# First attention of a two-layer block: probabilities times context, then Wv, instead of V; two kinds of transposition moved from TensorE to DMA

## What is computed

```python
q = (x @ Wq + bq)            # 16 heads of 128
k = (ctx @ Wk + bk)          # 4 key heads of 128, each used by 4 query heads
v = (ctx @ Wv + bv)          # 4 value heads of 128
q, k = rmsnorm(q), rmsnorm(k)
probs = softmax(q @ k.T / sqrt(128) + mask)
x = x + (probs @ v) @ Wo
```

## Time and profile before

| | us |
|---|---|
| runs of the kernel before, median (lowest to highest) | 5748.51 (5746.48 to 5749.6) |
| the profiled execution | 5724.92 |
| its span in the profile | 5723.2 |
| busy in the span: TensorE matmul | 4635.3 (81%) |
| TensorE weight load | 3681.8 (64%) |
| VectorE | 3950.1 (69%) |
| ScalarE | 2792.3 (49%) |
| GpSimd | 1760.5 (31%) |

### The profile page before, as it was taken

The page is one execution under the profiler, slowest core; times in us unless marked ns, Lnnn a source line. Parts: engine busy times, 40 slices in busy tenths (PEclk is TensorE's granted clock), DMA queues, the critical chain, the costliest instruction groups (busy, mean ns, idle before and its releaser), DMA issues. The chain is left out here.

```text
span 5723.2 us, 119501 instructions
## 1 busy us (share of the span) xinstructions
PE 4635.3 (81%) x39954; PEld 3681.8 (64%) x39955; DVE 3950.1 (69%) x7266; ACT 2792.3 (49%) x5207; POOL 1760.5 (31%) x2107
## 2 busy tenths in 40 slices
PE   4679999999999999999997407743888888888865
PEld 2447777777777777777776306632666666666654
DVE  4757777777777777777764633356777777777767
ACT  2335555555555555555543133321666666666643
POOL 2544444444444444444430163344000000000003
PEclk9789999999999999999998659975999998989976
DMA  5222112112212211221204274444333333333320
GB/s 191 89 62 57 38 49 57 50 42 52 52 41 51 57 48 44 52 52 40 52 27 122 76 217 124 124 128 116 93 86 87 83 87 81 90 78 89 89 52 24
DMA packets 395261, 436.41 MB, mean 76 GB/s; under 512 B 184225, under 2 KB 352801, under 8 KB 384526
## 3 DMA queue, kind: packets, MB, share of 16 engines
q1 hardware_dynamic: 366558, 388.13, 26.2%
q0 software_dynamic: 9216, 22.03, 1.2%
q10 hardware_dynamic: 19008, 19.40, 1.0%
HBM read 187.81 MB, written 144.83 MB: 58 GB/s over the span
## 5 line engine op out<-in xcount | busy, mean ns | idle before, releaser
L1804 DVE TENSOR_SCALAR_CACHE_REDUCE b_pr<-b_ps 112x1500 f32<-112x1500 f32 x256 | 439.3, 1716 | 279.4 <-PE b_ps L1879 279.1
L701 POOL TENSOR_TENSOR a_ksq<-a_kb 125x512 f32<-125x512 f32 x384 | 399.0, 1039 | 708.8 <-DVE a_kb L651 708.5
L616 ACT ACTIVATE a_pTh<-a_pt 125x448 f16<-125x448 f32 x768 | 402.7, 543 | 326.0 <-PE a_pt L775 321.4
L1761 ACT ACTIVATE b_pTh<-b_pt 125x448 f16<-125x448 f32 x768 | 392.7, 542 | 340.4 <-PE b_pt L1892 336.3
L673 DVE CUSTOM_DVE_ANT_0 a_pr<-a_ps,a_mask 112x1500 f32<-112x1500 f32 x256 | 439.7, 1718 | 164.7 <-PE a_ps L112 162.8
L110 PE MATMUL a_po<-a_vh,a_pTh 125*112 125x128 f16 x3072 | 549.5, 220 | 3.7 <-DVE a_pTl L689 3.1
L112 PE MATMUL a_po<-a_vh,a_pTl 125*112 125x128 f16 x3072 | 547.4, 219 | 0.0
L111 PE MATMUL a_po<-a_vl,a_pTh 125*112 125x128 f16 x3072 | 547.0, 219 | 0.0
L1811 DVE TENSOR_TENSOR b_pTl<-b_pt,b_pTh 125x448 f16<-125x448 f32 x768 | 454.0, 616 | 72.6 <-ACT b_pTh L1761 69.2
L1892 PE MATMUL b_pt<-ident,b_pr 112*125 112x112 f32 x3072 | 474.4, 294 | 32.0 <-DVE b_pTl L1811 26.9
L1997 POOL PARTITION_ALL_REDUCE f_ma<-f_mx x1 | 0.4, 374 | 1588.3 <-DVE f_mx L2057 1588.3
(11 more groups left out here) (376 smaller groups left out, 13470.8 us busy)
## 6 DMA issues: line engine op xcount, KB each, us to landing
b_ks<-b_kn SPq DMA_DIRECT2D x384, 187.5 KB, 4.4
scratch_cT<-a_cT SPq DMA_DIRECT2D x128, 375.0 KB, 3.1
b_cT<-scratch_cT SPq DMA_DIRECT2D x32, 1500.0 KB, 6.9
a_ctx<-ctx SPq DMA_DIRECT2D x32, 1440.0 KB
scratch_yd<-e_y SPq DMA_DIRECT2D x88, 256.0 KB, 2.1
scratch_xd<-q_zero ACTq DMA_DIRECT2D x4, 4736.0 KB
scratch_o<-a_ot SPq DMA_DIRECT2D x64, 224.0 KB
m_ot<-scratch_o SPq DMA_DIRECT2D x16, 896.0 KB
```

The source lines that it names most:

```text
L616: nc.scalar.activation(pTh[:, r % 2, 4 * third:4 * third + 4].rearrange("p k c -> p (k c)"), ps_t[n % 2][0:KP, 0:4 * RP], ACT.Copy).then_i ...
L701: nc.gpsimd.tensor_tensor(ksq[:, kt % 2], kb[0:KP, kt % 4], kb[0:KP, kt % 4], ALU.mult).then_inc(s["k_squared"], 1)
L1804: nc.vector.tensor_scalar(pr[:, n % 2].rearrange("p (a k) -> p a k", k=500), ps_s[0:RP, :, 0:500], -1.0, None, ALU.mult, ALU.min, accum_ou ...
```

## The change

Only the first attention and what reads its results are rewritten.

- There is no V any more. With the probabilities turned, step `P` (24 per batch, 12 matmuls of 224 columns each) multiplies them by the context itself, giving for each key head and its two rounds a mix of 256 features by 224 rows (`a_pa`). Step `G` splits this into `a_ah`, `a_al`, step `O` multiplies it by Wv (6 matmuls of 224 columns, 4 times per batch), and step `Z` adds bv and splits the result in f16, already turned, into `a_ot`. One store per two batches writes `scratch_oT`.
- The probabilities are scaled by one over the sum and split in their untransposed form: `H` on ScalarE and `L` on VectorE, each over 112x1500 from SBUF, 8 per batch. Then SyncE issues two DMA transpositions per round, from SBUF to SBUF (112 rows of 1536 f16 values).
- The context is loaded in four pieces of three rows per partition, split by `D` (ScalarE and GpSimd, 125x768, 4 per batch), and turned by four DMA transpositions per batch (128 rows of 1536 values). It is kept in f16 for three batches, since `P` needs it.
- TensorE loses `C`, `U`, `T`, `V` and keeps `K`, `R`, `S`. Key norms run over two tiles at once. GpSimd has an order of its own. The helper `rounds` writes six batches into one pass of the loop, 4 passes.
- `mix0_phase` loads the turned, split result directly and has no `turn_o` and no `split_o`.
- The second attention reads `scratch_cT` in another layout with 128 keys per tile; its matmul counts stay.

```diff
 ORDER0 = {
     "tensor": """
-        S0 T23< K0 V21< C1 V22< V23< T0 U0 K1 T1 T2 C2 S1 R0 U1 V0 V1 K2 C3 T3 T4 U2 R1 S2 V2 C4 T5 K3 V3 R2 V4
...
+        P17< K0 S0 K1 P18< S1 P19< K2 K3 S2 R0 O2< P20< P21< P22< K4 K5 P23< R1 S3 P0 R2 P1 P2 P3 K6 P4 R3 K7
+        S4 R4 P5 K8 S5 K9 P6 R5 S6 P7 P8 P9 P10 O3< R6 K10 O0 K11 R7 S7 P11 R8 P12 P13 R9 P14 P15 P16 O1 R10
+        R11""",
     "scalar": """
...
+        S0 H0 S1 H1 R0 Z2< S2 H2 D0 D1 G3< R1 R2 S3 H3 R3 D2 D3 R4 G0 S4 H4 S5 R5 H5 S6 Z3< R6 H6 Z0 R7 G1 R8
+        S7 R9 H7 Z1 R10 R11 G2""",
     "vector": """
...
+        S0 K1 I0 Q0 S1 L0 K2 I1 K3 S2 L1 R0 Q1 Z2< I2 K4 K5 L2 S3 G3< R1 Q2 R2 I3 K6 L3 R3 K7 S4 R4 G0 K8 I4
+        Q3 S5 L4 K9 I5 R5 S6 L5 Q4 I6 Z3< R6 K10 L6 Z0 K11 R7 S7 Q5 G1 R8 I7 R9 L7 Z1 R10 R11 G2 K0>""",
+    "gpsimd": """
+        D0 D1 N2 q6 D2 q7 D3 N3 q8 q9 N4 q10 q11 N5 q0> q1> N0> q2> q3> N1> q4> q5>""",
...
 def attn0_phase(nc, g, io):
...
+            def turn_ctx(tile, half):
...
+                wait(sp, s["work_done"], NW * (G - 1) + AT["K", HT * half + HT - 1] + 1)
+                passed(sp, sp_gate)
+                wait(sp, kept[half], 16 * G)
+                passed(sp, sp_gate)
+                sp.wait_ge(s["c_lo"], 4 * G + 2 * half + 2)
+                passed(sp, sp_gate)
+                for n, c in enumerate((ch, cl)):
+                    sp.dma_start_transpose(out=cT[:, n, part].rearrange("p k c q -> p (k c) q"),
+                                           in_=c[:, k, part].rearrange("q k d -> q (k d)")).then_inc(c_turned[half], 16)
...
+            def turn(tile, r):
+
+                G, h, k = tile[0], r // 2, r % 2
+                wait(sp, s["mix_done"], NKV * G + h - 1)
+                passed(sp, sp_gate)
+                for n, (p, pT, ready) in enumerate(((ph, pTh, "p_hi"), (pl, pTl, "p_lo"))):
+                    sp.wait_ge(s[ready], NR * G + r + 1)
+                    passed(sp, sp_gate)
+                    sp.dma_start_transpose(out=pT[:, h % 2, :, k], in_=p[:, k].rearrange("q k c -> q (k c)"))\
+                        .then_inc(turned[n][k], 16)
...
+                elif kind == "H":
+                    act.wait_ge(s["inv_ready"], NR * b + n + 1)
+
+                    wait(act, turned[0][n % 2], 16 * (NKV * b + n // 2))
+                    nc.scalar.activation(ph[:, n % 2, :, 0:KP], pr[:, n % 2].rearrange("p (k c) -> p k c", c=KP),
+                                         ACT.Copy, scale=inv[:, par, n:n + 1]).then_inc(s["p_hi"], 1)
...
                 if kind == "S":
                     dve.wait_ge(s["scores_done"], NR * b + n + 1)
+
+                    wait(dve, s["p_lo"], NR * b + n - 1)
...
+                elif kind == "L":
+                    dve.wait_ge(s["p_hi"], NR * b + n + 1)
+
+                    wait(dve, turned[1][n % 2], 16 * (NKV * b + n // 2))
+                    nc.vector.scalar_tensor_tensor(pl[:, n % 2, :, 0:KP],
+                                                   pr[:, n % 2].rearrange("p (k c) -> p k c", c=KP),
+                                                   inv[:, par, n:n + 1], ph[:, n % 2, :, 0:KP], ALU.mult,
+                                                   ALU.subtract).then_inc(s["p_lo"], 1)
...
+                elif kind == "P":
+                    h, c, third = n // 6, n // 3 % 2, n % 3
+                    ring, _ = of_three(batch)
+                    if n % 6 == 0:
+
+                        wait(pe, s["mix_lo"], NKV * b + h - 1)
+                        for t in turned:
+                            for k in range(2):
+                                pe.wait_ge(t[k], 16 * (NKV * b + h) + 16)
+                    for kt in range(4 * third, 4 * third + 4):
+                        feat = slice(c * 128, c * 128 + 128)
+                        last = three_products(nc, ps_a[h % 2][:, c], ch[0:KP, ring, kt, feat], cl[0:KP, ring, kt, feat],
+                                              pTh[0:KP, h % 2, kt].rearrange("p r q -> p (r q)"),
+                                              pTl[0:KP, h % 2, kt].rearrange("p r q -> p (r q)"),
+                                              start=(kt == 0), stop=(kt == KT - 1))
...
 def mix0_phase(nc, g, io):
...
-                wait(sp, s["oT_done"], 4 * t - 4)
-                sp.dma_start(ot[:, k, :], io.o0[ds(t * TT, TT), :]).then_inc(o_in[k], 16)
+                wait(sp, s["y_done"], t - 1)
+                sp.dma_start(oT[:, k].rearrange("p n h q -> p (n h q)"),
+                             io.oT[ds(t, 1)].rearrange("a p n h q -> p (a n h q)")).then_inc(o_in[k], 16)
```

More of the change, by code:

```diff
@@ L459, in batches, with moved, rounds, turn @@
         turn((g_, g_ % 2, g_ // 2))
+RING = 3
+ROUND = 2 * RING
+def moved(tile, d):
+    n, k, i = tile
+    return n + d, (k + d) % ROUND, i + (k + d) // ROUND
+def rounds(eng, steps, attend, work):
+    def turn(batch):
+        for kind, n, off in steps:
+            lead = {"D": 2, "K": 1, "R": 1, "q": 1, "N": 1, "Q": 1}.get(kind, 0)
+            at = moved(batch, off + lead)
+            if exists(at, B):
+                (work if lead else attend)(kind, n, at)
+    count = (B - 4) // ROUND
+    for b in (-2, -1, 0):
+        turn((b, b % ROUND, b // ROUND))
+    with eng.Fori(0, count) as i:
+        for k in range(1, ROUND + 1):
+            turn((ROUND * i + k, k % ROUND, i + k // ROUND))
+    for b in range(ROUND * count + 1, B + 1):
+        turn((b, b % ROUND, b // ROUND))
+def of_two(tile):
+    n, k, i = tile
+    return k % 2, RING * i + k // 2
+def of_three(tile):
+    n, k, i = tile
+    return k % RING, 2 * i + k // RING
 def attn0_phase(nc, g, io):
@@ new lines, in store, with load, step @@
+            def store(pair):
+                sp.wait_ge(s["o_taken"], 2 * NKV * pair + 2 * NKV)
+                passed(sp, sp_gate)
+                sp.dma_start(io.oT[ds(pair, 1)].rearrange("a p n h q -> p (a n h q)"),
+                             ot[:].rearrange("p n h b q -> p (n h b q)")).then_inc(stored, 16)
+            def load(tile, p):
+                if exists(tile, B):
+                    load_ctx(tile, p)
+            def step(tile):
+                after, second = moved(tile, 1), moved(tile, 2)
+                more = exists(second, B)
+                turn(tile, 0)
+                turn(tile, 1)
+                if exists(after, B):
+                    load_q(after)
+                turn(tile, 2)
+                load(second, 2)
+                load(second, 3)
+                turn(tile, 3)
+                if more:
+                    turn_ctx(second, 0)
+                turn(tile, 4)
+                turn(tile, 5)
+                if more:
+                    keep_ctx(second, 0)
+                if tile[1] % 2 == 0 and not (isinstance(tile[0], int) and tile[0] == 0):
+                    store(of_two(moved(tile, -1))[1])
+                turn(tile, 6)
+                load(moved(tile, 3), 0)
+                turn(tile, 7)
+                load(moved(tile, 3), 1)
+                if more:
+                    turn_ctx(second, 1)
+                    keep_ctx(second, 1)
@@ L795, in mix0_phase @@
+            rounds(pe, order["tensor"], attend, work)
 def mix0_phase(nc, g, io):
```

492 lines of the change are left out of this document (236 added, 256 removed).

## The result

The changed kernel takes **5340.24 us** (median of 4 runs, 5333.4 to 5348.59) against 5749.05 in the runs beside it: ratio 0.929, 95% interval 0.9274 to 0.9306, so 7.1% faster. The forecast was 5275 in a range of 5195 to 5620. Its side and range held; 65 us of the expected saving are missing, and the question of the experiments is where they went.

A forecast was written before the change was run, and what follows sets the result against it. TensorE was taken as the bound: 66.0 us a batch plus 1.1, 0.5 and 1.5 gave 69.1 against 83.5. Attention -446, start +10, end +10 and projection -50 gave 5275 us, range 5195 to 5620.

The forecast's parts named there:

- TensorE's price of P and O: First attention: new matmuls of 224 columns cost 0.0965 us each, 30.1 us a batch.
- rival 4: First attention: P's weight loads don't hide, 0.130 us a matmul, period 80 us, kernel 5600; chance 0.03.
- SyncE's issues and the transposition's DMA time: First attention, per batch: transpositions out of SBUF, priced from a DRAM one, take 33.5 us issue and 33.8 us DMA.
- Rivals 1 and 3: SBUF transpositions: issue at twice the price bounds SyncE, 5515, chance 0.12; or three times the DMA price, 6770, chance 0.12.
- The tightest chain: First attention, before P0: softmax and transposition take about 16 us while TensorE has 16.3 us of other work; no slack.
- Rival 2: First attention: new gaps before P at all four heads, 4 us each, cancel the attention's gain, 5735; chance 0.05.
- Output projection: After the attentions: a tile falls from 10.4 to 7.3 us without turn_o, 50 us saved (20 to 65).
- The start: Before the first attention's batches: clearing a_ch and a_cl on GpSimd adds 10 us (-10 to +25).
- the end: First attention's last batch has nothing to hide its DMA and softmax chain behind: adds 10 us (0 to 20).
- GpSimd had 39 us; ... again about 39: First attention, GpSimd per batch: key passes stay, half the powers go, four D come, so load stays about 39 us.
- I allow 1.5 us a batch for new gaps: First attention, TensorE: allowance for P waiting if the tightest chain doesn't fit, 1.5 us a batch (0 to 6).
- The sum: Whole kernel: -446 attention, +10 start, +10 end, -50 projection, so -476 us from the profiled 5724.9.

The follow-up runs named there:

- e1: Changed kernel with L computed from one SBUF input, the high part's subtraction left out (low part not right); 5178.15 us, ratio 0.8991 to the kernel before.
- e2: Changed kernel with GpSimd's power taken over 2 of the 8 values (keys not normed rightly); 5210.22 us, ratio 0.906 to the kernel before.
- e7: Changed kernel with one-input L, and ahead of it a second one-input operation over 750 columns into a spare buffer; 5242.56 us, ratio 0.9107.

## Why the prediction was right, and what it missed

- **TensorE's price of P and O.** Taken 0.0965 us between 128 and 512 columns (the line itself gives 0.0963). The rows of 36 matmuls in a line:

```profile
1500.35 0.26 PE L110 MATMUL a_pa<-a_pTh,a_ch 125*128 125x224 f16 x1
...
1503.71 0.26 PE L112 MATMUL a_pa<-a_pTh,a_cl 125*128 125x224 f16 x1
```

  (1503.71 - 1500.35) / 35 = 0.096. Held; rival 4 (weights that don't hide, 0.130) is out.
- **SyncE's issues and the transposition's DMA time.** The term that was known least:

```profile
L620 SPq DMA_TRANSPOSE a_pTh<-a_ph x256: 1301/1358/2214, 384.2 to 2696.6; - x128
...
L590 SPq DMA_TRANSPOSE a_cT<-a_cl x64: 1446/1898/3243, 308.2 to 2580.9; - x64
```

  The round's issue was taken at 1.63 and is 1.36 us; the context's at 1.86 and is 1.90. The round's land in 3.1 us at the median, the context's in 4.7. The price of 1.64 us of all 16 engines lies between the 1.5 and the 2.1 to 2.2 of the experiments, and the share of 0.67 is near the forecast's 70%. The cost out of SBUF is near that of the row from DRAM, not that of the copy. Rivals 1 and 3 are out for this kernel; with 36 transpositions a batch both mechanisms show. The round's issue of 1.36 us is above the row's 1.24 and below the 1.63 of its size, so it came shorter than it was taken.
- **The tightest chain** (16 against 16.3 us) fitted: TensorE waits 2.1 us in all for a transposition that P needs. Rival 2 is out.
- **Output projection.** Forecast 7.3 us a tile, measured 7.33; 50 saved, measured 47 without the first `turn_o`. The start came 5 us later (first score at 376.4 for 371.6), forecast +10. From the last score to the projection's first matmul it is 39.5 us for 34.6, so the end costs 5, forecast +10.
- **The step that failed** is "GpSimd had 39 us; ... again about 39". It is 0.704 x 73.2 = 52 us. From the rows above: 6 powers are 9.9 where "half of the powers go" made them 6; four D are 6.7, about what the sentence set against the other half of the powers; and 12 x (0.39 + 0.21) = 7.2 us are products and squares standing while L runs. With it falls "I allow 1.5 us a batch for new gaps", which looked for them in front of P. They came in front of R, where keys are turned, by a chain that I hadn't drawn: the sum for two tiles at once, one power for both, and two products. Not all of it is GpSimd's: 0.9 us a batch is the store of `a_ot`, a wait that the sum didn't have either. The terms for waits were mis-sized by 73.2 - 69.1 = 4.1 us a batch, 31 x 4.1 = 127 us, of which 32 came back elsewhere: the start 5 better than taken, the end 5, the phases behind about 12, the projection 3 worse, and 13 between the first score and the last, where 332.7 us are saved and not the 319 of 31 x 10.3.
- **VectorE and ScalarE.** L was priced at 1.72 and costs 1.78 when nothing stands in its way, 1.87 at the mean. The price was right, and what it would hold, and what would hold it, was not asked.
- **The sum.** Profiled execution against profiled execution, 381 us were saved where the sum said 476: 95 are missing, 127 in the batches, less 32. By medians it is 5340 against 5275, since that of before lies 24 us above its profiled run and that of the changed kernel 3.5 below. 5340 lies in the forecast's own range of 5200 to 5360, and there is luck in it: without the 32 us that other terms gave back it would be 5372. e1, in which L is short, has a period below the forecast one: 68.9 by the count of the experiments, 67.8 by that of the forecast's 69.1.

## What to carry to other kernels

When a change adds a VectorE pass from SBUF like the L of this kernel, look at what GpSimd does at that time, and add the pass to GpSimd's load: here GpSimd's products and squares, 1.04 us alone, took 1.43 and 1.25 at the mean in the kernel with the two-input L of 1.78 us, and 1.13 and 1.15 in e1 with the one-input L of 1.0; a busy share summed engine by engine doesn't show it. A batch of work that is halved in number and doubled in size (here the powers) is to be priced from its own size, and its chain drawn to the engine that waits. Before a step is moved forward in a written order, ask which buffers the steps that it passes set free: one entry of an order cost 3.6 points here, and two more buffers gave most of it back. Where a buffer is stored in one piece and then filled again, look at who waits for the store.

## What the runs showed of the hardware that was not expected

- A transposition by DMA out of SBUF, 112x1536 values of two bytes: 1.36 us to issue, 3.1 us to landing, 1.5 us of all 16 engines when one is left out and 2.1 to 2.2 when one is added. With 36 per batch of 79.5 us the DMA share is 1.04 and SyncE waits only 118 of 2000 us; with 28 (share 0.90) TensorE waits 0.8 us in 2000 for them.
- GpSimd's power takes 0.70 us for 2 values a partition (median; 0.90 at e2's mean, with the holds by L), 1.01 for 4 and 1.64 for 8: about 0.16 us for each value, over some 0.4.
- A `tensor_scalar` of VectorE from f32 in SBUF to f16 runs 1500 columns in 1.0 us and 750 in 0.6, and holds a GpSimd product or square that starts while it runs, as the two-input form does. It is itself held by one that started before it: 1.66 us at the median of e7's second pass.
